# First attention over the context: three blank fills moved from the head of the load queue into the fifth step of its loop

## What is computed

```
x = x + _L0_attn_ref(_layernorm(x), ...)                  # complex decay mixer and MLP
x = x + _L0_xattn_ref(_layernorm(x), ctx_1024, ctx_1024, ...)   # 16 heads of 16: the first attention over the context
x = x + _L0_ffn_ref(_layernorm(x), ...)                   # 32 experts, top 4, capacity 250
x = x + _L1_attn_ref(...); x = x + _L1_xattn_ref(...); x = x + _L1_ffn_ref(...)
```

```
pos = jnp.cumsum(onehot, axis=0)[jnp.arange(N * K), flat_e] - 1
keep = pos < capacity
buf = jnp.zeros((E + 1, capacity, d)).at[e_s, p_s].set(xf[tok])[:E]
h = silu(einsum('ecd,edh->ech', buf, wg)) * einsum('ecd,edh->ech', buf, wu)
routed = jnp.zeros_like(xf).at[tok].add(contrib)
```

## Time and profile before

| what | us |
|---|---|
| median of 3 runs | 1769.85 |
| lowest and highest of them | 1769.07, 1772.64 |
| the profiled execution, its own time | 1773.58 |
| span of its instructions | 1771.5 |
| of it, the third stage (attention and experts) | about 317 to 1024 |
| of it, the attention's loop on PE | about 339 to 598 |

### The profile page before, as it was taken

The page is one execution under the profiler, slowest core; times in us unless marked ns, Lnnn a source line. Parts: engine busy times, 40 slices in busy tenths (PEclk is TensorE's granted clock), DMA queues, the critical chain, the costliest instruction groups (busy, mean ns, idle before and its releaser), DMA issues. The chain is left out here.

```text
span 1771.5 us, 30415 instructions
## 1 busy us (share of the span) xinstructions
PE 1483.0 (84%) x11654; PEld 1116.7 (63%) x11654; DVE 781.7 (44%) x2196; ACT 696.2 (39%) x1472; POOL 461.7 (26%) x437
## 2 busy tenths in 40 slices
PE   3989887589888899999999935898699999819992
PEld 2556554366666667888888823555466676519991
DVE  4665662356676332222222225776466676411111
ACT  1543543556656311222222212556565556403330
POOL 0221210001233544666666410111101111040003
PEclk9999998689999899999999967999899999959996
DMA  6433422977675214778777634455666667139992
GB/s 247 131 94 118 149 89 87 168 124 136 118 124 95 80 30 116 193 199 202 200 198 195 145 107 98 99 126 126 110 132 114 111 115 121 22 114 361 343 340 82
DMA packets 255033, 254.98 MB, mean 144 GB/s; under 512 B 117532, under 2 KB 228468, under 8 KB 249396
## 3 DMA queue, kind: packets, MB, share of 16 engines
q1 hardware_dynamic: 210868, 222.04, 49.6%
q0 software_dynamic: 41152, 28.50, 8.7%
q10 hardware_dynamic: 2880, 2.62, 0.4%
HBM read 195.67 MB, written 57.20 MB: 143 GB/s over the span
## 5 line engine op out<-in xcount | busy, mean ns | idle before, releaser
L2643 PE MATMUL cross_ps_score<-cross_q,cross_k 128*128 128x250 f32 x1024 | 223.5, 376 | 0.8 <-DVE cross_q L3063 0.8
L2643 PEld LDWEIGHTS cross_ps_score<-cross_q,cross_k 128*128 128x128 f32 x1024 | 195.5, 191 | 23.9 <-DVE cross_q L3063 1.0
L3072 DVE TENSOR_TENSOR cross_prob<-cross_act_,cross_ps_score 128x250 f32<-128x250 f32 x128 | 53.2, 416 | 268.3 <-ACT cross_act_ L2786 268.3
L3151 POOL DMA_INDIRECT x_sum<-cross_ye,cross_token x64 | 128.6, 2010 | 80.6 <-ACT cross_ye L2792 68.5
L2813 DVE TENSOR_REDUCE cross_nmax<-cross_ps_score 100x2 f32<-100x722 f32 x128 | 111.8, 902 | 72.3 <-PE cross_ps_score L2420 67.5
L1656 ACT ACTIVATE layer_parts<-layer_ps_prob 128x400 f32<-128x400 f32 (+1 forms) x192 | 97.0, 508 | 103.7 <-PE layer_ps_prob L1479 102.1
L2673 ACT ACTIVATE cross_prob<-cross_ps_prob 128x400 f32<-128x400 f32 (+1 forms) x192 | 96.2, 507 | 101.2 <-PE cross_ps_prob L2453 99.6
L2655 PE MATMUL cross_ps_prob<-cross_val,cross_prob 128*125 128x256 f32 x512 | 115.8, 379 | 0.0
L2786 ACT ACTIVATE cross_act_<-cross_ps_score 128x250 f32<-128x250 f32 x128 | 48.6, 380 | 167.6 <-PE cross_ps_score L2643 166.3
L2655 PEld LDWEIGHTS cross_ps_prob<-cross_val,cross_prob 128*125 128x125 f32 x512 | 93.5, 188 | 12.8
L3141 POOL DMA_INDIRECT cross_xe<-ln_rows,cross_token x64 | 79.8, 1247 | 81.7 <-PE cross_ps_misc L2629 57.4
(11 more groups left out here) (404 smaller groups left out, 2941.4 us busy)
## 6 DMA issues: line engine op xcount, KB each, us to landing
experts_w<-in_w SPq DMA_DIRECT2D x40, 1024.0 KB
k_stack<-mixer_part SPq DMA_DIRECT2D x32, 541.5 KB, 3.9
cross_k<-in_wg SPq DMA_DIRECT2D x32, 512.0 KB
cross_k<-in_wu SPq DMA_DIRECT2D x32, 512.0 KB
cross_val<-in_wd SPq DMA_DIRECT2D x32, 512.0 KB
layer_stacks<-k_stack SPq DMA_DIRECT2D x32, 270.8 KB
cross_k<-k_stack SPq DMA_DIRECT2D x27, 270.8 KB
mixer_ctx<-in_ctx_t POOLq DMA_DIRECT2D x16, 361.0 KB, 3.8
```

The source lines that it names most:

```text
L2643: ins = nc.tensor.matmul(ps_pre[m][:, side, 0:CAP], w[s][:, k, m * P:(m + 1) * P], xt[s][:, k, :], start=(k == 0), stop=(k == KD - 1))
L3151: g.indirect_dma_start(prog.x_sum, bass.IndirectOffsetOnAxis(token[:, 2 * e + t:2 * e + t + 1], 0), ye[s][:, t, :], None, compute_op=ALU.a ...
```

## The change

The three fills leave the head of SP's stream and are issued in step b = 4 (`BLANKS_AT = G`), behind `load_half(6, 0)` and ahead of `store_rows(3)`, with the same waits for the memsets of their source tiles. POOL's wait for `zeroed` moves from before its loop to step b = 8, just ahead of the first scatter; its wait for `blank_sums` moves up beside that for `blank_rows`, ahead of the first gathers. No transfer, size or tile changes.

```diff
+    BLANKS_AT = G
...
-                sp.wait_ge(zero_set, 1)
-                sp.dma_start(prog.row_token[0:SLOTS0].rearrange("(p n) o -> p (n o)", p=T),
-                             blank[:].rearrange("p n o -> p (n o)")).then_inc(zeroed, 16)
-                sp.wait_ge(blank_set, 1)
-                sp.dma_start(prog.ln_rows[N:N + CAP].rearrange("(t p) d -> p t d", p=HALF), xe[0][:]).then_inc(blank_rows, 16)
-                sp.dma_start(prog.x_sum[N:N + CAP].rearrange("(t p) d -> p t d", p=HALF), xe[0][:]).then_inc(blank_sums, 16)
                 for b in range(B):
...
                         load_half(b + 2, 0)
+                    if b == BLANKS_AT:
+                        sp.wait_ge(zero_set, 1)
+                        sp.dma_start(prog.row_token[0:SLOTS0].rearrange("(p n) o -> p (n o)", p=T),
+                                     blank[:].rearrange("p n o -> p (n o)")).then_inc(zeroed, 16)
+                        sp.wait_ge(blank_set, 1)
+                        sp.dma_start(prog.ln_rows[N:N + CAP].rearrange("(t p) d -> p t d", p=HALF), xe[0][:]).then_inc(blank_rows, 16)
+                        sp.dma_start(prog.x_sum[N:N + CAP].rearrange("(t p) d -> p t d", p=HALF), xe[0][:]).then_inc(blank_sums, 16)
                     if b > 0:
                         store_rows(b - 1)
...
-                g.wait_ge(zeroed, 16)
                 for b in range(B):
                     if b + 1 < B:
                         set_base(b + 1)
+                    if b == 2 * G:
+                        g.wait_ge(zeroed, 16)
...
                 g.wait_ge(blank_rows, 16)
+                g.wait_ge(blank_sums, 16)
...
-                g.wait_ge(blank_sums, 16)
```

## The result

The changed kernel took 1765.89 us (median of 8 runs, 1762.39 to 1768.38) beside 1770.09 us for the kernel before (8 runs, 1768.86 to 1773.57): a ratio of 0.9973 with a 95% interval of 0.9962 to 0.9983. It is faster by some 4 us, inside my range and on the forecast side, but 3.4 us above my 1762.5. Run again beside the kernel before it had 0.9981 (0.9969 to 0.9993) and 0.9975 (0.9963 to 0.9988). The three together say 0.9976, a gain of about 4.2 us where I forecast 7.3.

A forecast was written before the change was run, and what follows sets the result against it. PE bounds the kernel, standing still for sequence 2's late keys and then running at half clock. Gains of 4.8 + 2.6 less 0.1 give 7.3 us, from 1769.85 to 1762.5; range 1760.2 to 1767, the forecast's own 1761 to 1764.5.

The forecast's parts named there:

- What bounds, and where the loss sits: PE bounds; its one DMA wait in 340 to 600 us, 6.3 us before sequence 2's first scores, also halves the clock.
- Part 1: Attention loop's head: without fills ahead, sequence 2's half 0 keys land at 354.1, 4.8 us gained, 1.5 us idle left.
- Part 2: First to fourth pair of sequence 2's scores: TensorE's clock no longer halves, 2.6 us gained, 0 as the other end.
- it stays up: At sequence 2's first scores the clock holds 2.4 GHz through 1.5 us of idle time, as PE resumes before 355.08.
- The row of 340 to 342: Sign for the clock holding: PE worked 0.91 us of 2.00 there and the clock stayed at 1.00.
- rival (a): Clock falls all the same at sequence 2's scores, its gain lost wholly or half; gain 4.7 to 6.0 us; chance 0.17.
- Part 3: Fills in step 4 may delay sequence 7's half 0 keys: cost 0.1 us, 1.5 as the far end.
- (b): Fills at the head cost their bytes alone, 3.5 us; 2.8 us idle remain and the clock falls: 1766.4; chance 0.09.
- (c): SP issues sequence 2's loads so early that no idle time is left; 6.34 + 2.6 us gained: 1760.9; chance 0.07.
- (e): Nothing comes of it: something other than queue length, such as busy DRAM, holds sequence 2's keys: 1769.8; chance 0.07.
- (d): Wait moves to step 4, sequence 7's half 0 late: 1773.9 in full, chance 0.03; 1765.5 in part, chance 0.04.

The follow-up runs named there:

- the dose: Against the kernel before, only the x_sum fill moved to step 4; slot table and ln_rows fills stayed at the head: ratio 0.9994.
- the shape: Kernel before with its two large fills still at the head but written as 128 rows of 2000 bytes from 128 partitions: ratio 0.9986.
- the runs with 0.13 us: Changed kernel with sequence 2's half 0 keys issued ahead of its src and x in step 0: ratio 0.9953, again 0.9963.
- products in the gap: Needless PE products where it waits for sequence 2's keys: 7 in the changed kernel, ratio 0.996; 20 in the kernel before, ratio 1.001.

## Why the prediction was right, and where its sizes were off

**What bounds, and where the loss sits:** right. The one DMA wait in the loop shrank, and all the gain that stays from profile to profile lies between the stage's first load and the fourth pair of scores.

**Part 1, the landing: 4.8 forecast, 4.2 measured** (42.14 to 37.94; 4.0 between the two repeats). The mechanism was right, as the dose and the shape show. The step that missed is "without fills, sequence 1's x lands at 342.87 - 0.4". POOL's bases in the changed kernel, beside the earlier trace rows:

```profile
335.15 0.72 POOL L3089 TENSOR_TENSOR cross_base<-cross_xin,cross_bias_sum 100x256 f32<-100x256 f32 x1 [35.14 <-DMA cross_xin<-x_after]
347.45 0.72 POOL L3089 TENSOR_TENSOR cross_base<-cross_xin,cross_bias_sum 100x256 f32<-100x256 f32 x1 [11.58 <-DMA cross_xin<-x_after]
```

From 347.45 to PE's start at 358.86 the four loads of sequence 2 took 11.41 us: the forecast's 11.3. But from 335.15 to 347.45, the four loads of sequence 1, which no fill ever stood ahead of, took 12.30 where I had 11.3 from the trace of before. The direction holds in every profile: from the last semaphore update of sequence 0's x to that of sequence 1's, the five with fills from few partitions at the head took 10.6 to 11.7 us and the eight with no fill there 11.9 to 12.8. The size varies, for each group spreads by about 1 us. So these loads run somewhat faster when such fills stand behind them, and slower when another full load does. The run with the fills in step 0 says the same from the other side: keys with fills behind them landed 0.7 us sooner. I had allowed 0.3 for this, and looked for it behind the fills instead of ahead of them. Why loads ahead in the queue should care is not shown; that few engines work on the fills and leave the others' share of memory free is my reading. With the fills over all engines behind them these loads took 11.8 us, between the two groups, which leaves it open.

**Part 2, the clock: 2.6 forecast, 1.3 measured against the first profile of before, 0.2 against the second** (6.49 or 5.39, to 5.19). The price of the fall was right: 3.84 was the stretch I took at full clock, 3.74 and 3.76 came out. What failed is "it stays up". I argued that the clock had fallen 2.5 us into the idle time, and that PE would be at work before that. It was, after 2.2 us, and the clock fell none the less, while PE was already busy. The fall comes late: in the ten profiles with one it stands 2.4 to 3.4 us after PE had run out of work, whether PE was still idle or had resumed 0.5 to 1.35 us before. So "2.5 us into the idle time" was not the idle time that it takes, and PE's start did not forestall it. Even 1.43 us of idle time (fills in step 0) were followed by a fall; in the runs with 0.13 us, or with products in the gap, there was none. Between 0.13 and 1.43 us nothing was run. The row of 340 to 342 was no witness: the two gaps there are 0.63 and 0.88 us, with work between. So rival (a) happened, in its milder half, near the price I gave it (a gain of 4.7 to 6.0; the head gained 4.2 to 5.5, the runs say 4.2), and I had put 0.17 on it where the wait's own error made it the likelier case.

And the first profile of before flattered the change: the clock was down for 10.2 us in it and for 6.8 in the repeat, for the same wait. A loss read off one execution's clock can shrink by that much in the next.

The Trainium skill (page "TensorE: Matmul & The Clock Gate", section "HAM oscillation — how this bites in real kernels") warns of idle gaps of PE only from a certain length on. The gaps of 2.2 and 1.4 us here are shorter than that and were followed by a fall, so they do not agree with it, and the measurement decides.

**Part 3, step 4: 0.1 forecast, nothing measured.** The store of rows 3 and the next one in the changed kernel:

```profile
417.00 0.29 SPq L2345 DMA_DIRECT2D ln_rows<-cross_xf  x1
...
432.37 0.29 SPq L2345 DMA_DIRECT2D ln_rows<-cross_xf  x1
```

15.37 us, against 15.38 in the kernel before (418.38 in the earlier trace rows to 433.76). PE's first scores of sequence 7 start at 433.74 without a wait. No rival at that place had anything to it.

**The rivals.** (a) came true in part. (b) is refuted twice: the fills cost more than 3.5 us as they are (4.0 to 4.2), and 1.4 us when spread, less than their bytes at 163 GB/s. (c) and (e) did not happen. (d) did not happen, nor at step 0 where it was provoked.

**The sum.** 4.2 + 1.3 + 0 = 5.5 by the pair of profiles I argued from, 4.0 + 0.2 = 4.2 by the repeated pair; the runs say 4.2. Of the 3.1 us by which I was too high, some 0.6 to 0.8 lie in the landing and 1.3 to 2.4 in the clock. That the result lies in the range is owed to its upper part, which I had drawn over rivals (a) and (b); the forecast's own 1761 to 1764.5 does not hold it.

## What to carry to other kernels

A store without hurry, set ahead of urgent loads in a full queue, costs what its slowest DMA engine takes, so look at its shape as well as at its size: 500 KB written as 500 short rows from 125 partitions held the queue for three times as long as 256 longer ones from 128. Before you move such a store, see if a reordering of what stays (here the keys ahead of src and x) is worth as much, and do both. And price a short stall of PE with the clock behind it: shortening the stall from 6.3 to 2.2 us left a fall of the clock; only the kernels with no wait left, or with products in it, kept 2.4 GHz.

## What the runs showed of the hardware that I had not expected

- TensorE's clock can fall after PE has resumed: with 1.9 to 2.2 us of idle time it went to 1.2 GHz 0.5 to 0.8 us into the new work, with 1.43 us of it 1.35 us into it. The stretch of work behind took 5.18 to 5.19 us, and 3.74 to 4.32 where the clock stayed up.
- A fill from 125 partitions was counted in by five semaphore updates and one from 128 by sixteen; 500 KB of the first kind landed in 4.2 us, of the second in 1.4.
- The same loads, in the same order, took 10.6 to 11.7 us where a fill from few partitions was queued behind them, and 11.9 to 12.8 where another load was.
- The kernel before, with not one instruction changed, took 116.0 us for steps 8 to 14 in one profile and 109.9 in the next, which is more than the change under study is worth.
